# Token loop of a cross-attention and expert kernel: normalised rows split to fp16 in SBUF and turned by a transposing DMA

## What is computed

```
x = x + xattn(layernorm(x), ctx, mask, Wq, Wk, Wv, Wo, bo)     # 16 heads of 64
x = x + ffn(layernorm(x), w1, w2, w3, new_w1, ..., gate)       # 9 experts, hidden 704
xattn: softmax((q @ Wq)(ctx @ Wk).T / 8, masked) @ (ctx @ Wv) @ Wo + bo
ffn:   scores = sigmoid(x @ gate.T + bias); the best 2 of 9, their scores normalised to sum 1
       out = sum over the two of weight * ((silu(x @ w1.T) * (x @ w3.T)) @ w2.T)
```

## Time and profile before

| | us |
|---|---|
| median of 3 runs | 422.93 (422.58 to 423.85) |
| the profiled execution | 422.82 |
| its span | 421.0 |
| PE busy in the span | 403.9 |
| DVE, ACT, POOL busy | 275.2, 253.2, 246.9 |

### The profile page before, as it was taken

How to read it: one execution, slowest core, us unless ns; L and a number is a source line. 1 busy time by engine, 2 the same in 40 slices (tenths; PEclk the granted TensorE clock), 3 DMA queues, 4 the chain that set the end, 5 groups by cost and what they waited for, 6 DMA issues and landing times.

```text
span 421.0 us, 10140 instructions
## 1 busy us (share of the span) xinstructions
PE 403.9 (96%) x3176; PEld 307.2 (73%) x3176; DVE 275.2 (65%) x683; ACT 253.2 (60%) x444; POOL 246.9 (59%) x214
## 2 busy tenths in 40 slices
PE   8999999999999999789899999999999999999991
PEld 7777677778877877776677777777777777777781
DVE  1777989999899988987889854444444444444430
ACT  3759899999999986724655444444444444444430
POOL 6536789998999888253245534445444444444232
PEclk9999999999999999989999999999999999999997
DMA  7994456576575666256789978989889989989742
GB/s 228 342 321 132 132 160 201 161 189 201 155 235 166 177 187 190 74 151 120 154 138 139 146 131 133 141 139 129 150 141 142 141 139 140 143 134 153 119 68 36
DMA packets 106512, 66.03 MB, mean 157 GB/s; under 512 B 80992, under 2 KB 99808, under 8 KB 106464
## 3 DMA queue, kind: packets, MB, share of 16 engines
q1 hardware_dynamic: 98784, 54.90, 57.4%
q0 software_dynamic: 7680, 10.49, 16.5%
HBM read 36.23 MB, written 9.96 MB: 110 GB/s over the span
## 4 chain that ended last, share of the span: by engine, by line
PE 56%; issue 16%; DMA 14%; DVE 4%; POOLq 4%; POOL 3%; SPq 1%; ACT 0%; DVEq 0%
PE ps L824 12%; PE ps L621 12%; PE ps L651 11%; DMA out_rows<-work,idx_all 9%; PE ps L844 7%; PE ps L634 4%; POOLq L1709 3%; PE ps L558 3%; POOL work L1700 3%; PE ps L617 2%; DMA w_all<-in_wv 2%; PE ps L523 1%; DMA work<-work 1%; PE ps L667 1%; DMA work<-xn_rows,idx_all 1%
## 5 line engine op out<-in xcount | busy, mean ns | idle before, releaser
L824 PE MATMUL ps<-w_all,work 128*128 x960 | 150.1, 313 | 0.8 <-DVE work L1447 0.5
L824 PEld LDWEIGHTS ps<-w_all,work 128*128 128x128 f16 x960 | 93.6, 98 | 47.0 <-issue 1.2
L1721 POOL DMA_INDIRECT out_rows<-work,idx_all x40 | 64.2, 1606 | 102.5 <-ACT work L1076 101.1
L1516 DVE SCALAR_TENSOR_TENSOR work<-ps,work 128x352 f32<-128x352 f32 x80 | 41.2, 523 | 66.4 <-PE ps L824 66.3
L844 PE MATMUL ps<-w_all,work 128*128 x681 | 80.8, 273 | 1.1 <-DMA work<-work 1.1
L844 PEld LDWEIGHTS ps<-w_all,work 128*128 128x128 f16 x681 | 66.3, 98 | 12.0 <-issue 1.6
L1641 POOL TENSOR_TENSOR w_all<-stage,w_all 128x1088 f16<-128x1088 f32 x31 | 69.9, 2256 | 6.5 <-ACT w_all L916 6.2
L1055 ACT ACTIVATE work<-ps 128x352 f32<-128x352 f32 x80 | 36.8, 463 | 53.6 <-PE ps L824 53.6
L1061 ACT ACTIVATE work<-work 128x704 f16<-128x704 f32 x39 | 30.8, 790 | 62.2 <-DVE work L1516 62.2
L1700 POOL DMA_INDIRECT work<-xn_rows,idx_all x40 | 40.6, 1014 | 29.9 <-issue 10.3
L621 PE MATMUL ps<-w_all 128*128 128x462 f16 (+1 forms) x288 | 57.4, 336 | 0.0
(11 more groups left out here) (159 smaller groups left out, 537.2 us busy)
## 6 DMA issues: line engine op xcount, KB each, us to landing
stage<-in_wt SPq DMA_DIRECT2D x36, 544.0 KB, 4.4
work<-in_x SPq DMA_DIRECT2D x30, 128.0 KB, 3.7
out_rows<-work SPq DMA_DIRECT2D x18, 128.0 KB, 4.3
xn_rows<-work SPq DMA_DIRECT2D x18, 128.0 KB, 4.1
w_all<-in_x SPq DMA_DIRECT2D x1, 1536.0 KB, 14.6
work<-work SPq DMA_TRANSPOSE x78, 3.6
w_all<-in_wq SPq DMA_DIRECT2D x4, 256.0 KB, 6.8
w_all<-in_wv SPq DMA_DIRECT2D x2, 512.0 KB, 8.2
```

The lines of the kernel that those rows point to most:

```text
L824: mm = pe.matmul(ps[:, c, 0:half], xt[:, t % 2, block, :], weights(wbase + off, half), start=(k == 0 and n == 0), stop=(k == KD - 1 and n ...
L1516: dve.scalar_tensor_tensor(out=sg[:, t % 2, cols], in0=ps[:, 2 + c, 0:HID // 2], scalar=1.0 / SP_W, in1=sg[:, t % 2, cols], op0=ALU.mult, ...
L1721: pool.indirect_dma_start(out=acc, out_offset=bass.IndirectOffsetOnAxis(ap=idx_all[:, t:t + 1], axis=0), in_=yb[:, t % 2], in_offset=None, ...
```

## The change

Tiles 0 to 2 stay as they are (X_PE = 3). For tiles 3 to 15 the two transposes on PE, `x_high` on ACT and `x_low` on DVE go. In their place, at the end of step n of each engine: ACT writes the high fp16 part of the normalised rows of tile n+2 into `xn16` (`norm_high`, 128 x 256, SBUF to SBUF, behind `exp(n)`), POOL subtracts it from `xnb` into the low part (`norm_low`, 128 x 256, behind `rstd(n-3)`), and SP, at the head of its step n+1, waits for that and issues a transposing DMA of 128 x 512 fp16 into `x_h` and `x_l` (`turn_x(n+2)`), ahead of `load_x(n+3)`. `xn16` lies on the bytes of `xbuf` (same offset ROUTE, same buffer number), so `load_x(i)` also waits until tile i-2 is turned. `scores` waits for the DMA. No line of the diff touches how the offset of the normalisation (`nmr`) is formed.

```diff
-        x_h, o = lview(o, [2, KD, P], F16)
-        x_l, o = lview(o, [2, KD, P], F16)
+        x_hl, o = lview(o, [2, 2 * KD, P], F16)
+        x_h, x_l = x_hl[:, :, 0:KD], x_hl[:, :, KD:2 * KD]
...
+        xn16, _ = view(work, ROUTE, [2, 2 * D], F16)
...
+        def x_turned(eng, i):
+
+            if i >= X_PE:
+                eng.wait_ge(nt_in[i % 2], 16 * ((i - 1) // 2))
...
             def load_x(i):
                 at_least(sp, xn_ok, i - 1)
+                x_turned(sp, i - 2)
...
+            def turn_x(i):
+
+                sp.wait_ge(nl_ok, i - X_PE + 1)
+                sp.wait_ge(sc_mm, 3 * (i - 1))
+                sp.dma_start_transpose(out=x_hl[:, i % 2], in_=xn16[:, i % 2]).then_inc(nt_in[i % 2], 16)
+
             def step(n):
+                if on(n, -1) and n + 1 >= X_PE:
+                    turn_x(n + 1)
...
             def scores(i):
-                pe.wait_ge(xl_ok, i + 1)
+                pe.wait_ge(xl_ok, min(i + 1, X_PE))
+                x_turned(pe, i)
...
-                elif on(n, -1):
-                    norm_turn(n + 1)
...
             def normalise(i):
-                at_least(act, xt_mm, i - 1)
+                at_least(act, xt_mm, min(i - 1, X_PE))
+                at_least(act, nl_ok, i - 1 - X_PE)
...
+            def norm_high(i):
+
+                act.wait_ge(xn_ok, i + 1)
+                act.activation(xn16[:, i % 2, 0:D], xnb[:, i % 2], ACT.Copy).then_inc(nh_ok, 1)
...
-                if on(n, -1):
-                    x_high(n + 1)
...
                 if on(n, 0):
                     exp(n)
+                if on(n, -2):
+                    norm_high(n + 2)
...
-                if on(n, -1) and n not in (0, 1):
-                    x_low(n + 1)
...
+            def norm_low(i):
+
+                pool.wait_ge(nh_ok, i - X_PE + 1)
+                pool.tensor_tensor(xn16[:, i % 2, D:2 * D], xnb[:, i % 2], xn16[:, i % 2, 0:D],
+                                   ALU.subtract).then_inc(nl_ok, 1)
...
                 if on(n, LAG_X1):
                     rstd(n - LAG_X1)
+                if on(n, -2) and n + 2 >= X_PE:
+                    norm_low(n + 2)
```

More of the change, by code:

```diff
@@ L279, in build @@
         cut_ok, max8_ok = sem("cut_ok"), sem("max8_ok")
+        nh_ok, nl_ok, nt_in = sem("nh_ok"), sem("nl_ok"), sems("nt_in", 2)
         x0_mm, x0h_ok, x0l_ok = sem("x0_mm"), sem("x0h_ok"), sem("x0l_ok")
@@ L295, in build @@
         WARM, WARM_IDS, WARM_OUT, WARM_X0 = 30, 30, 16, 10
+        X_PE = 3
         def on(s, lag):
             return 0 <= s - lag < NT
+        def x_turned(eng, i):
+            if i >= X_PE:
+                eng.wait_ge(nt_in[i % 2], 16 * ((i - 1) // 2))
         def cap(n):
@@ L602, in norm_turn @@
                 pe.wait_ge(xn_ok, i + 1)
-                at_least(pe, lg_ok, i - 1 - LAG_G)
                 at_least(pe, xl_ok, i)
@@ L657, in gate_turn @@
                 at_least(pe, lg_ok, i)
-                pe.wait_ge(xl_ok, cap(i + LAG_G + 2))
-                pe.wait_ge(xh_ok, cap(i + LAG_G + 2))
+                pe.wait_ge(xl_ok, X_PE)
                 for k in range(KD):
@@ L972, in step @@
                     w_high(W_PRE - 1)
+                    norm_high(3)
                     b_high(3)
@@ L1450, in drain @@
             def drain():
-                dve.wait_ge(xt_mm, NT)
+                x_turned(dve, NT - 2)
+                x_turned(dve, NT - 1)
                 dve.memset(r["s16a"][:, K1, :], 0.0)
```

## The result

The changed kernel takes 423.94 us (median of 20 runs, 422.78 to 425.43) against 423.18 us (20 runs, 421.91 to 423.85) of the kernel before on the same chips: ratio 1.0027, 95% interval 1.0017 to 1.0038. By the medians it is slower by 0.8 us, by the ratio by 1.1 us, where 1.1 us were forecast to be won. The profiled execution has a span of 421.8 us (before 421.0).

A forecast was written before the change was run, and what follows sets the result against it. The loop was taken as bound by the number of PE instructions, other engines narrowly keeping up. 2.86 - 1.5 - 0.3 = 1.06 us gained, so a median of 421.9 us, with a range from 420.0 to 425.4.

The forecast's parts named there:

- Removed on PE: PE, tiles 3 to 15: the two transposes cost 0.22 us a pair; 13 pairs save 2.86 us.
- `norm_low` 0.68 us: POOL: added operation of 0.68 us, 8.42 us of work a step; POOL ends step 9 at 117.5 us, before at 115.6.
- `norm_high` against `x_high`: ACT: exchanging one copy for the other costs 0 to 0.22 us a step, taken as 0.
- the term of the stall: PE: 1.5 us of waiting for x or weights made late by POOL, counted as one delay, and 0.3 us for DMA.
- the rings through x and the weights: SP and ACT after POOL's late step 9: x costs PE 1.3 us, weights 1.5; one delay, taken as 1.5 us.
- rival B: SP: `load_x` behind `turn_x` closes a ring longer than PE's step over steps 4 to 12; 425.2 us, chance 0.26.
- the weight ring: Late `w_low` in step 9 holds back a weight load, 2.6 us late for ACT; 1.5 us for PE.
- The path that I priced for it: `load_x(12)` issued at about 118.75, landing in 4.0 us, 2.8 us late for ACT's `normalise(12)`; 1.3 us left for PE.
- DMA, 0.3 us: DMA engines: each transpose adds 0.79 us a step and stretches landings; 0.3 us more delay, bounds 0 to 0.79.
- Rival A: PE keeps all of its 2.86 us if POOL's `norm_low` takes 0.4 us; 420.1 us, chance 0.22.

The follow-up runs named there:

- e10_no_first: e8_best4 without the two `rstd_first` bursts in steps 5 and 9, so statistics of tiles 8 to 15 are left out: 419.96 us, ratio 0.9918 to the kernel before.
- e1_order: The changed kernel with `load_x` issued ahead of `turn_x` on SP: 422.60 us, ratio 0.9999 to the kernel before.
- e3_xpe4: The changed kernel with tile 3 too turned on PE (`X_PE = 4`): 422.67 us, ratio 0.9994 to the kernel before.
- e8_best4: The changed kernel with three repairs: `load_x` ahead of `turn_x`, tile 3 on PE, clamp as a reduction: 421.79 us, ratio 0.9984 to the kernel before.
- e7_cut: The changed kernel with DVE's clamp of the router logits done as a reduction: 424.37 us, ratio 1.0036 to the kernel before.
- e4_xpe12: The changed kernel with only tiles 12 to 15 turned by DMA (`X_PE = 12`): 422.75 us, ratio 0.9996 to the kernel before.
- e13_six: e8_best4 with only tiles 9, 10 and 12 to 15 turned by DMA: 422.49 us, ratio 0.9976 to the kernel before.
- e2_dve: The changed kernel with the low part formed on DVE instead of POOL and `turn_x` behind the stores on SP: 428.31 us, ratio 1.0127 to the kernel before.

## Why the prediction was wrong

- **Removed on PE, 0.22 us a pair:** right. Steps without a wait have 8.04 and 8.65 us (8.26 and 8.87 before).
- **`norm_low` 0.68 us, POOL at 8.42 us a step and behind by up to 2 us in steps 5 and 9:** right in size (0.67 us; 8.92 of 9 us busy) and in place. That this lag governs is shown for what is left after the repairs (e10_no_first); in the changed kernel POOL heads the chain of step 6, and in step 10 its `w_low` is what the clamp ended with. The gaps of the earlier trace rows are in seven other steps, not six, and steps 6 and 10 have next to none either (0.09 us at most): there POOL was still making up for the burst.
- **`norm_high` against `x_high`, 0:** right, 0.40 us each.
- **The step that failed is the term of the stall.** I put 1.5 us for the rings through x and the weights, as one delay that reaches PE once, in step 10, and 0.3 for DMA: 1.8 us. Measured are 3.9 us, in three places with three paths:
  - Steps 3 and 4, 0.89 us. I had the ring `turn_x`, `load_x`, `normalise`, `exp`, `norm_high`, `norm_low` in rival B only, for steps 4 to 12 and landings over 4.5 us, and in the sum half a microsecond for `exp` in step 2. The ring turned once, in step 2 (POOL waited 1.46 us), and nothing covered it: 0.83 us in step 3, which both e1_order and e3_xpe4 take away.
  - Steps 6 and 7, 1.71 us. This is the weight ring, near the size that I gave it (1.5), but behind the burst of step 5. I took the largest delay once, behind the burst of step 9, and said that it doesn't grow; it was through at step 6 already. That the two bursts make two delays is seen in e8_best4, 0.94 us in step 6 and 0.53 in step 10.
  - Step 10, 1.28 us. The path that I priced for it isn't there: x of tile 12, which I had 2.8 us late, was issued at 120.75, landed in 2.4 us where I had 4.0, and lay there 0.7 us before `normalise` began at 123.90; nor did ACT wait for weights in that step. What PE waited for was `residual` behind the clamp. DVE's clamp waiting for POOL's `w_low` is in no row of the kernel before except as one longer instance (0.60 us in step 5), since there the clamp met `rstd`'s small operations. POOL's delay moved a long one under it. Without the lock (e7_cut) 0.58 of the 1.28 us stay, by the lag, and 0.81 come up in step 12. In step 6 the lock has next to no part in the changed kernel (1.56 to 1.45 without it); in e1_order it has. How much of 1.34 and 1.14 us in e1_order is the lock can't be said to the tenth, since e8_best4 (0.94 and 0.53) differs from it by tile 3 too.
- **DMA, 0.3 us:** wrong sign if anything. Landings got shorter, and no wait of PE goes back to the transfer of a transpose; the 1.29 us that SP takes to issue one are in the ring of step 2. A transpose cost 0.67 us of the 16 engines, not 0.79.
- **Rival A:** it wanted `norm_low` at 0.4 us, and it took 0.67.
- **Rival B, slower through the ring at 425.2:** the sign was that of B, the mechanism mostly not. The landing was 2.6 us, so the ring was 6.8 us long (an estimate by B's own terms) and never the bound after its first turn.
- **The range** held the time (420.0 to 425.4), as it was wide enough for losses by another mechanism; the forecast of a gain did not hold.

## What to carry to other kernels

When one of several nearly full engines gets more work, count its time over the whole loop against the shortened period, bursts included, before counting what the bound engine saves: here 0.67 us a step on POOL took back more than 0.22 us on PE gave. Moving work off PE paid in full only in steps where the engine that took it had a gap (e4_xpe12, e13_six). And an engine that shifts in time can meet another one in a shared resource: look for instructions whose length varies in the trace, not only for waits, since such a block is booked as busy time.

## What the runs showed of the hardware

- A DVE operation on 9 elements with one SBUF source and a constant took up to 2.18 us (e3_xpe4) while POOL's `w_low` of 128 x 1088 ran, and 0.17 to 0.23 us beside POOL's operations on 1 or 4 elements. All 18 instances over 0.3 us, in seven kernels, ended 0.02 to 0.03 us behind such a `w_low`. A reduction over 18 elements from SBUF at the same place took 0.17 us every time.
- A DVE subtraction of 128 x 256 with both operands in SBUF took 0.36 to 1.58 us in e2_dve, the one with an operand in PSUM 0.41 us.
- A transposing DMA of 128 x 512 fp16 landed in 2.5 to 3.8 us in the loop and took 0.67 us of the 16 DMA engines, in packets of 256 bytes; the x loads and the stores of the same stretch, in packets of 1024 bytes, took 0.46 us for 128 KB.
- A 128 KB load landed in 2.6 us (median) when it was issued apart from the 544 KB loads, against 4.8 us right behind one.
